# Another order of the graph layers, two of them prepared late, and shared pieces of two graphs from the 17th step on

## The chip, the core and the metric

The kernel runs on one core of a Trainium2 chip. The core has five engines, each with its own in-order queue: PE (TensorE, matmuls and transposes), DVE (VectorE), ACT (ScalarE), POOL (GpSimd) and SP (SyncE, which starts DMAs). They meet only at semaphores: an instruction waits until a counter has reached a constant. The metric is the time of one execution on the device, in microseconds (us), as the median of several runs. All times below are in us unless marked otherwise.

## What is computed

Four graphs of 256 nodes each go through two graph attention layers, then through a mixture of experts. `_L0_xattn_ref` is the attention part, `_L0_ffn_ref` the experts.

```python
def gat_layer(x, adj, W, a_self, a_neigh, b):       # 256 nodes, 8 heads of 32
    feat = jnp.einsum('nf,hfo->hno', x, W)
    attn_self = jnp.einsum('hno,ho->hn', feat, a_self)
    attn_neigh = jnp.einsum('hno,ho->hn', feat, a_neigh)
    e = jax.nn.leaky_relu(attn_self[:, :, None] + attn_neigh[:, None, :], 0.2)
    e = e + MASK_VAL * (1.0 - adj)[None, :, :]
    alpha = jax.nn.softmax(e, axis=-1)
    out = jnp.einsum('hnm,hmo->hno', alpha, feat) + b[:, None, :]
    return jax.nn.elu(jnp.transpose(out, (1, 0, 2)).reshape(out.shape[1], -1))

x = x + jnp.tanh(g_xattn[0]) * two_gat_layers(ctx_512, adj=_layernorm(x))
x = x + jnp.tanh(g_ffn[0]) * experts(_layernorm(x))
```

`experts` picks for each of the 1024 tokens two of eight experts by a router, and adds two shared experts through which every token goes (gate and up projection to 640, silu, product, down projection).

## The kernel before

**The stream of steps.** A layer of a graph is cut into four steps (`UNITS = 4`): two halves of the rows by two groups of four heads. `ORDER` lists the eight pairs (graph, layer) in the order in which they run; L is the place in it, and step w = 4 L + u belongs to layer place L. There are 32 steps (0 to 31). In a second layer the input is the first layer's output of the same graph, `h0_t[n]`. What one step needs of each engine:

- PE: `scores` makes the attention scores (bf16, in ps_z), `turn` transposes the exponentiated scores (8 transposes, ps_pt), `weigh` multiplies them with the features (ps_o).
- ACT: `copy_scores` copies ps_z to SBUF, `exponent` takes four exponentials with row sums, `copy_turned` copies ps_pt.
- DVE: `mask_max` applies the leaky relu and mask and takes the row maxima (one wide instruction and four custom ones).

The work of a step overlaps with that of others: PE makes the scores of step w + 4 while it turns step w, ACT copies the scores of step w + 3 and exponentiates step w + 1, DVE takes the maxima of step w + 3.

**Once per layer.** `score_nodes` (PE, ps_t) and `split_scores` (DVE, three bf16 parts) prepare the scores, `features` (PE, ps_f) and `copy_features` (ACT) the features: one layer ahead. At the end of a layer `invert_sums` (DVE), `spread_inverse` (PE, ps_f), `copy_inverse` (ACT), then `divide` (DVE), `elu_exponent` (ACT) and `end_elu` (DVE) give its output, in steps 0 and 1 of the next layer. Behind a second layer come `turn_h1` (PE), `add_attention` and `normalise` (DVE, with a power on POOL), `turn_x_norm` (PE) and `copy_x_norm` (ACT), then the routing: `router` (PE), `router_exponent` (ACT), `choose` twice (DVE), `ranks` (PE) and `place` (DVE). POOL then scatters the token rows to the experts' slots in memory (`send_rows`).

**The shared experts as fillers.** Per graph there are ten pieces (`PIECES`): `gate_up` on PE (eight matmuls in the trace), a tanh on ACT and two products on DVE (`silu_up`), which write `hidden`. Four down steps (`down`, ten matmuls in the trace) follow. `filler_slots` puts two of these a step between the parts of the attention steps. Graph 0's fourteen slots stood in steps 21 to 28, each piece in the one bank ps_gu, so that a piece waits for the DVE products of the piece before it (`hid_ready`). Graph 1's first five pieces stood in steps 29 to 31, its other five and its downs behind the loop, and these rotated through three banks (ps_gu and the halves of ps_z), which are free since scores come only up to step 27's slot; there a piece waits only for the third piece before it. Behind the loop graphs 2 and 3 follow with all their pieces and downs. Between them stand the small steps of routing.

**Then the routed experts.** 23 tiles of 128 tokens go through gate, up and down with the weights of their expert (`step`, `gate_chunk`, `down_tile`). PE's first routed matmul ends the part that this change touches. It needs the table of tiles (`make_table`, DVE), a tile read back from memory, and the weights of all experts; five experts' weights are loaded late, since their place in SBUF holds the attention's buffers until graph 3 is normalised and the rows of graphs 0 and 1 are sent.

`mask_stats` (DVE) and `make_mask` (POOL) make a graph's mask; `project_second` (DVE) makes the projected attention vectors of the second layers.

## Time and profile before

| | us |
|---|---|
| median of 3 runs | 446.31 (446.15 to 446.85) |
| profiled execution, its own time | 445.5 |
| span of its trace | 443.7 |
| start of the turn of step 17 | 95.00 |
| start of the turn of step 21 (first filler step) | 111.88 |
| start of the turn of step 29 | 171.20 |
| end of the last weigh (step 31) | 187.60 |
| first routed matmul on PE | 267.02 |
| PE busy | 395.6, 89% of the span |

The trace is of one execution. The span leaves out what lies around the first and last instruction, so the execution's own time is 1.8 longer. A line of it names the engine, the source line (L598 is line 598), the operation, what it writes and reads, and how long the engine had stood idle before it and for whom it had waited. Busy time of PE is a little too large, since the modelled ends of matmuls overlap the next start; starts are the better ruler. The names in the rows are those of the tensors in the program, and most of the attention's buffers lie in `weights`.

### The profile page before, as it was taken

Reading aid. Unit: us, or ns where it says so; the run is one execution under the profiler, and the core shown is the slowest. Engines: PE = TensorE matmul, PEld = TensorE weight load, DVE = VectorE, ACT = ScalarE, POOL = GpSimd, SP = SyncE. Lnnn points to the kernel's source line nnn. Section 1 sums busy time; section 2 is a strip of 40 time slices with the busy share of each in tenths; the row PEclk is TensorE's granted clock in tenths of the full one; section 3 lists DMA queues with packets and bytes.
Section 4 is the critical chain, followed back from the end, with each engine's and each line's share of the span. In section 5 each row is a group of like instructions: output and inputs, shape, how many; then the busy total and the mean of one; then the engine's idle time right before and its main releaser. Section 6 shows DMA issues by size and latency. Waiting matters only on the chain.

```text
span 443.7 us, 7225 instructions
## 1 busy us (share of the span) xinstructions
PE 395.6 (89%) x2295; PEld 289.1 (65%) x2296; DVE 257.2 (58%) x814; ACT 205.5 (46%) x519; POOL 90.5 (20%) x100
## 2 busy tenths in 40 slices
PE   3877787787988999997999999999999999999991
PEld 2445464555765878776888886666667676766660
DVE  3799999899887784785474424343333333433330
ACT  4597999999854668420120213232232323232320
POOL 6656140001000022121312000212121212121221
PEclk9998999999998999998999999999999999999997
DMA  6199999100000001000698300122212222221212
GB/s 172 27 353 343 339 354 429 60 1 1 1 1 1 2 7 67 1 24 27 242 429 347 88 2 24 26 36 38 36 38 39 35 46 33 39 36 24 24 12 24
DMA packets 22988, 42.48 MB, mean 96 GB/s; under 512 B 1968, under 2 KB 20976, under 8 KB 21680
## 3 DMA queue, kind: packets, MB, share of 16 engines
q1 hardware_dynamic: 17632, 35.76, 23.3%
q0 software_dynamic: 4080, 5.18, 7.4%
q10 hardware_dynamic: 1248, 1.18, 0.8%
q8 instruction: 16, 0.26, 0.2%
q14 instruction: 12, 0.10, 0.1%
HBM read 24.81 MB, written 17.31 MB: 95 GB/s over the span
## 4 chain that ended last, share of the span: by engine, by line
PE 59%; DVE 19%; ACT 14%; POOL 3%; issue 2%; DMA 2%; POOLq 0%; DVEq 0%
PE ps_z L749 13%; PE ps_o L775 11%; PE ps_gu L749 9%; ACT weights L843 6%; PE ps_pt L605 5%; PE ps_z L598 5%; DVE weights L1041 5%; PE ps_gu L598 4%; DVE weights L1036 3%; ACT weights L834 3%; ACT weights L849 3%; PE ps_pt L765 3%; PE ps_gu L605 2%; DVE hidden L1094 1%; DVE gate_silu L1091 1%
## 5 line engine op out<-in xcount | busy, mean ns | idle before, releaser
L439 POOL DMA_INDIRECT out<-y_sb,tile_in x23 | 35.9, 1559 | 166.1 <-DVE y_sb L1280 163.0
L843 ACT ACTIVATE weights<-weights 128x256 f32<-128x256 f32 x128 | 64.3, 536 | 0.1
L749 PE MATMUL ps_z<-weights,tile_t 128*128 x184 | 63.2, 486 | 0.0
L775 PE MATMUL ps_o<-weights,hidden 128*128 x230 | 53.5, 380 | 0.9 <-ACT hidden L950 0.9
L1091 DVE SCALAR_TENSOR_TENSOR gate_silu<-gate_tanh,ps_z 128x256 f32<-128x256 f32 x66 | 24.5, 371 | 49.5 <-ACT gate_tanh L935 36.2
L517 PE MATMUL ps_pt<-ident,weights 128*128 128x128 f32 x256 | 35.4, 284 | 15.6 <-ACT weights L849 15.2
L749 PEld LDWEIGHTS ps_z<-weights,tile_t 128*128 128x128 f32 x184 | 33.2, 190 | 23.2 <-issue 22.0
L775 PEld LDWEIGHTS ps_o<-weights,hidden 128*128 128x128 f32 x230 | 43.6, 190 | 7.0 <-issue 1.1
L935 ACT ACTIVATE gate_tanh<-ps_gu 128x256 f32<-128x256 f32 x23 | 8.8, 383 | 80.5 <-PE ps_gu L749 80.5
L517 PEld LDWEIGHTS ps_pt<-ident,weights 128*128 128x128 f32 x256 | 29.9, 147 | 22.6 <-issue 21.8
L1036 DVE SCALAR_TENSOR_TENSOR weights<-weights 128x1024 f32<-128x1024 f32 x32 | 39.0, 1219 | 9.1 <-ACT weights L834 5.6
L1091 DVE SCALAR_TENSOR_TENSOR gate_silu<-gate_tanh,ps_gu 128x256 f32<-128x256 f32 x43 | 18.0, 420 | 45.2 <-ACT gate_tanh L935 35.3
L749 PE MATMUL ps_gu<-weights,tile_t 128*128 x92 | 43.2, 592 | 0.0
L598 PE MATMUL ps_gu<-x_norm_t,weights 128*128 128x256 f32 x160 | 39.6, 391 | 4.1 <-DVE hidden L1094 4.1
L834 ACT ACTIVATE weights<-ps_z 128x1024 f32<-128x1024 f32 x32 | 33.5, 1047 | 8.7 <-PE ps_z L508 8.7
L598 PE MATMUL ps_z<-x_norm_t,weights 128*128 128x256 f32 x160 | 37.3, 382 | 0.0
L598 PEld LDWEIGHTS ps_gu<-x_norm_t,weights 128*128 128x128 f32 x160 | 29.7, 192 | 9.1 <-DVE hidden L1094 5.6
L386 POOL TENSOR_TENSOR weights<-weights,minus_half 128x2 f32<-128x2 f32 x8 | 7.5, 940 | 132.3 <-DVE weights L1010 132.3
L849 ACT ACTIVATE weights<-ps_pt 128x1024 f32<-128x1024 f32 x32 | 33.5, 1046 | 0.8 <-PE ps_pt L517 0.8
L598 PEld LDWEIGHTS ps_z<-x_norm_t,weights 128*128 128x128 f32 x160 | 29.8, 190 | 4.1 <-issue 0.4
L935 ACT ACTIVATE gate_tanh<-ps_z 128x256 f32<-128x256 f32 (+1 forms) x46 | 15.2, 330 | 34.7 <-PE ps_z L749 34.7
L505 PE MATMUL ps_z<-weights 96*128 96x512 bf16 x64 | 27.3, 426 | 4.3 <-DVE weights L1026 2.9
(192 smaller groups left out, 618.4 us busy)
## 6 DMA issues: line engine op xcount, KB each, us to landing
weights<-w_experts SPq DMA_DIRECT2D x8, 1920.0 KB, 14.1
slots<-pad_row SPq DMA_DIRECT2D x9, 1188.0 KB, 13.5
weights<-w_experts SPq DMA_DIRECT2D x1, 3840.0 KB, 14.5
tile_in<-slots SPq DMA_DIRECT2D x23, 132.0 KB, 2.1
out<-y_sb ACTq DMA_DIRECT2D x4, 256.0 KB, 2.2
weights<-x SPq DMA_DIRECT2D x2, 256.0 KB, 4.4
x_in<-x SPq DMA_DIRECT2D x2, 256.0 KB, 5.3
out<-y_sb,tile_in POOLq DMA_INDIRECT x23, 3.8
```

Of the source, the lines that this page charges most:

```text
L439: pool.indirect_dma_start(out=out, out_offset=bass.IndirectOffsetOnAxis(ap=tile_in[:, slot, ID_COL:ID_COL + 1].bitcast(U32), axis=0), in_= ...
L505: pe.matmul(ps_z[:, pair, :], v[0:PART_ROWS, half * P:(half + 1) * P], pick_self[0:PART_ROWS, h:h + 2, :], start=True, stop=False, skip_gr ...
L517: mm = pe.transpose(ps_pt[:, i * P:(i + 1) * P], logits[:, w % AHEAD, i * P:(i + 1) * P], ident)
L598: mm = pe.matmul(dst[:, part * N:(part + 1) * N], weights[:, a:a + P], x_norm_t[n % PAIR][:, k, :], start=(k == 0), stop=(k == KC - 1))
L605: mm = pe.matmul(dst, hid_shared[:, e, i, half * P:(half + 1) * P], weights[:, a:a + D], start=(e == 0 and i == 0), stop=(e == NSH - 1 and ...
L749: mm = pe.matmul(ps_chunk[c][:, 0:2 * cw], tile_t[:, r % 2, k, :], weights[:, bass.ds(off + (k * GU + 2 * c0), 2 * cw)], start=(k == 0), s ...
L775: mm = pe.matmul(ps_o[:, 0:D], hid_t[:, r % 2, i, :], weights[:, bass.ds(off + (KC * GU + i * D), D)], start=(i == 0), stop=(i == IC - 1))
L834: act.activation(logits[:, w % AHEAD, :], ps_z.rearrange("p a n -> p (a n)"), ACT.Copy).then_inc(z_copied, 1)
L843: ins = act.activation(v, v, ACT.Exp, bias=neg_max[:, w % AHEAD, i:i + 1], scale=-1.0, accum_out=sums[:, L % PAIR, s:s + 1])
L849: act.activation(probs_t[:, w % 2, :], ps_pt, ACT.Copy).then_inc(probs_copied, 1)
L1036: dve.scalar_tensor_tensor(out=z, in0=z, scalar=LEAK, in1=z, op0=ALU.mult, op1=ALU.max).then_inc(bent_ready, 1)
L1091: dve.scalar_tensor_tensor(out=gate_silu[:, s, 0:w], in0=gate_tanh[:, s, 0:w], scalar=1.0, in1=gate, op0=ALU.add, op1=ALU.mult).then_inc(r ...
```

## The change

`ORDER` becomes 00 10 01 20 11 30 21 31 (graph, layer), so that graph 0's second layer stands at place 2 rather than 3 and graph 1's at place 4 rather than 5. At places 2 and 7 a second layer now follows its own first layer with only one other between them. These two are `TIGHT`: their `score_nodes`, `split_scores` and `features` come in the steps right before them, and their scores are made two steps later than those of other layers, with their copies and maxima squeezed in behind. Graph 0's filler slots move from steps 21 to 28 to steps 17 to 24. Graph 1's thirteen first slots stand in steps 25 to 31, now all in the bank ps_gu as graph 0's, and one down step is left behind the loop. Behind the loop the small steps of routing are spread anew between the pieces of graph 2, and the ranks, place and table of graph 3 move behind the first pieces of graph 3. The statistics of graphs 2 and 3 move to steps 5 and 10, the second projection to step 1.

```diff
-ORDER = ((0, 0), (1, 0), (2, 0), (0, 1), (3, 0), (1, 1), (2, 1), (3, 1))
+ORDER = ((0, 0), (1, 0), (0, 1), (2, 0), (1, 1), (3, 0), (2, 1), (3, 1))
+TIGHT = tuple(L for L in range(2, STREAM) if ORDER[L][1] == 1 and ORDER[L - 2] == (ORDER[L][0], 0))
+NODES_AT = {UNITS * L - 3 if L in TIGHT else UNITS * (L - 1) - 1: L for L in range(PAIR, STREAM)}
+FEATURES_AT = {UNITS * L - 2 if L in TIGHT else UNITS * L - 3: L for L in range(PAIR, STREAM)}
+SPLIT_AT = {UNITS * L - 2 if L in TIGHT else UNITS * (L - 1): L for L in range(PAIR, STREAM)}
 def filler_slots(w):
     if w < FIRST_FILL:
-        return ()
-    if w < SECOND_FILL:
-        first = 2 * (w - FIRST_FILL) - 1
-        return tuple((0, s) if 0 <= s < PIECES + len(DOWNS) else None for s in (first, first + 1))
-    first = 2 * (w - SECOND_FILL) - 1
-    return tuple((1, s) if s >= 0 else None for s in (first, first + 1))
+        return None, None
+    n, at = (0, FIRST_FILL) if w < SECOND_FILL else (1, SECOND_FILL)
+    first = 2 * (w - at) - 1
+    return tuple((n, s) if 0 <= s < PIECES + len(DOWNS) else None for s in (first, first + 1))
+def scores_early(w):
+    if tight_step(w, -1):
+        return w + 2
+    if tight_step(w, 0):
+        return w + 3
+    return w + 4 if w % UNITS != 0 and is_free(w + 4) else None
+def scores_late(w):
+    if tight_step(w, -2):
+        return w + 2
+    if tight_step(w, -1):
+        return w + 3
+    return w + 4 if w % UNITS == 0 and is_free(w + 4) else None
...
# the loop on PE
-                if slots_now and slots_now[0]:
-                    filler(slots_now[0])
-                if u != 0 and w + UNITS < ALL_UNITS:
-                    scores(w + UNITS)
+                if first:
+                    filler(first)
+                if scores_early(w) is not None:
+                    scores(scores_early(w))
...
# the loop on ACT
-                if w + 3 < ALL_UNITS:
-                    copy_scores(w + 3)
+                if copy_early(w) is not None:
+                    copy_scores(copy_early(w))
...
+                if tight_step(w, -1):
+                    copy_turned(w)
+                    copy_scores(copy_late(w))
                 if w + 1 < ALL_UNITS:
                     exponent(w + 1)
-                if slots_now and slots_now[0] and slots_now[0][1] < PIECES:
-                    tanh_piece(*slots_now[0], piece_bank(*slots_now[0]))
+                if first and first[1] < PIECES:
+                    tanh_piece(*first, 0)
...
# behind the loop on DVE
             for n in range(PAIR, B):
                 for i in range(PIECES):
                     tail_piece(n, i)
-                    if n == PAIR and i == 6:
+                    if n == 3 and i == 0:
                         place(3, ps_o)
-                    if n == PAIR and i == 7:
+                    if n == 3 and i == 1:
                         make_table()
```

`tight_step(w, k)` is true where w lies k steps from the first step of a tight layer, `is_free` where a step belongs to no tight layer; `copy_early`, `copy_late` and `maxima` hold the same kind of table for ACT's copies and DVE's maxima. `turn_bank_free` holds the waits on the bank ps_t that stood in three places.

**The first tight layer, on ACT.** These are ACT's rows of steps 5 to 7, and the copy that opens step 8. ps_z is read by `copy_scores`, weights<-weights x4 is `exponent`, ps_pt is read by `copy_turned`, ps_f by `copy_features`. Before:

```order
L834 ACTIVATE weights<-ps_z 128x1024
L843 ACTIVATE weights<-weights 128x256 x4
L860 ACTIVATE att_exp<-weights 128x256 x2
L849 ACTIVATE weights<-ps_pt 128x1024
L834 ACTIVATE weights<-ps_z 128x1024
L830 ACTIVATE weights<-ps_f 128x512
L843 ACTIVATE weights<-weights 128x256 x4
L849 ACTIVATE weights<-ps_pt 128x1024
L834 ACTIVATE weights<-ps_z 128x1024
```

After:

```order
L888 ACTIVATE weights<-weights 128x256 x4
L905 ACTIVATE att_exp<-weights 128x256 x2
L894 ACTIVATE weights<-ps_pt 128x1024
L888 ACTIVATE weights<-weights 128x256 x4
L894 ACTIVATE weights<-ps_pt 128x1024
L879 ACTIVATE weights<-ps_z 128x1024
L875 ACTIVATE weights<-ps_f 128x512
L894 ACTIVATE weights<-ps_pt 128x1024
L879 ACTIVATE weights<-ps_z 128x1024
L888 ACTIVATE weights<-weights 128x256 x4
```

Steps 5 and 6 lose their copies of scores, and step 7 has two, with the copy of its turned weights between them and the exponents of step 8 behind.

**The second tight layer, on ACT.** Before, these are the rows of steps 29 (from its tanh) to 31 (up to its first tanh), with the pieces of graph 1 (gate_tanh):

```order
L876 ACTIVATE gate_tanh<-ps_gu 128x256
L880 DMA out<-y_sb 128x2x256
L843 ACTIVATE weights<-weights 128x256 x4
L876 ACTIVATE gate_tanh<-ps_z 128x256
L849 ACTIVATE weights<-ps_pt 128x1024
L876 ACTIVATE gate_tanh<-ps_z 128x256
L876 ACTIVATE gate_tanh<-ps_gu 128x256
```

After, the rows of steps 27 and 28, with pieces 3 to 5 of graph 1:

```order
L879 ACTIVATE weights<-ps_z 128x1024
L875 ACTIVATE weights<-ps_f 128x512
L894 ACTIVATE weights<-ps_pt 128x1024
L879 ACTIVATE weights<-ps_z 128x1024
L888 ACTIVATE weights<-weights 128x256 x4
L921 ACTIVATE gate_tanh<-ps_gu 128x256 x2
L879 ACTIVATE weights<-ps_z 128x1024
L900 ACTIVATE weights<-ps_f 128x512
L888 ACTIVATE weights<-weights 128x256 x4
L921 ACTIVATE gate_tanh<-ps_gu 128x256
L894 ACTIVATE weights<-ps_pt 128x1024
L879 ACTIVATE weights<-ps_z 128x1024
```

The first tanh of step 27 stands behind two copies of scores, a copy of features, a copy of turned weights and four exponents, and all pieces are in ps_gu.

**Behind the loop, on PE.** The counts are those of the program, half of the trace's. L598 (before) and L653 (after) are pieces, L605 and L660 downs, L566 and L621 the turn of graph 3's attention output, L543 and L598 (after) the turn of its normalised rows. Before:

```order
L598 MATMUL ps_gu<-x_norm_t1,weights 128x256 x4
L566 MATMUL ps_t<-ident,weights 128x128 x4
L598 MATMUL ps_z<-x_norm_t1,weights 128x256 x4
L578 MATMUL ps_f<-router_w,x_norm_t0 128x8 x4
L598 MATMUL ps_z<-x_norm_t1,weights 128x256 x4
L598 MATMUL ps_gu<-x_norm_t1,weights 128x256 x4
L543 MATMUL ps_t<-ident,rows30 128x128 x4
L605 MATMUL ps_pt<-weights,hidden 128x256 x10
```

After:

```order
L660 MATMUL ps_gu<-weights,hidden 128x256 x5
L653 MATMUL ps_z<-x_norm_t0,weights 128x256 x4
L621 MATMUL ps_t<-ident,weights 128x128 x4
L653 MATMUL ps_z<-x_norm_t0,weights 128x256 x4
L633 MATMUL ps_f<-router_w,x_norm_t0 128x8 x4
L653 MATMUL ps_gu<-x_norm_t0,weights 128x256 x4
L653 MATMUL ps_z<-x_norm_t0,weights 128x256 x8
L598 MATMUL ps_t<-ident,rows30 128x128 x4
```

The pieces between the small steps are now graph 2's (x_norm_t0), one more of them stands between the turn of the attention output and the turn of the rows, and of graph 1 (x_norm_t1) only one down step is left in front.

## Rows read from the trace of the kernel before

**Rows 1.** Busy time by stretch: engines in us, granted clock, share of DMA.

```profile
95.00:111.88 16.88, 14.13 (x144) 10.46 (x145) 16.05 (x49) 16.88 (x45) 1.32 (x2) 1.00 0.01 1
111.88:171.20 59.32, 55.17 (x405) 43.37 (x404) 44.58 (x155) 38.24 (x100) 5.69 (x6) 0.97 0.03 10
171.20:187.60 16.40, 16.23 (x147) 13.09 (x145) 10.89 (x34) 10.58 (x29) 1.28 (x2) 1.00 0.05 17
187.60:267.02 79.42, 75.43 (x369) 65.31 (x366) 42.56 (x163) 12.42 (x33) 13.11 (x15) 0.98 0.42 162
267.02:443.70 176.68, 166.31 (x666) 112.27 (x664) 61.73 (x162) 46.23 (x114) 35.85 (x23) 0.98 0.21 32
```

**Rows 2.** Chain of work that ended last, six pieces of it: start, us, what.

```profile
63.97 0.80 ACT att_exp L860 x2
...
67.06 1.97 ACT weights L843 x8
69.03 0.91 ACT weights L849
...
120.41 1.24 DVE weights L1036
121.67 1.47 DVE weights L1041 x8
...
217.48 1.73 PE ps_gu L598 x8
...
265.02 2.16 PE ps_pt L605 x10
```

**Rows 3.** Timeline of PE in step 17: start, us, line, operation, idle before.

```profile
95.00 1.06 PE L517 MATMUL ps_pt<-ident,weights 128*128 128x128 f32 x8 [1.29 <-ACT weights L849]
95.90 0.38 PE L505 MATMUL ps_z<-weights 96*128 96x512 bf16 x1
...
96.87 0.65 PE L532 MATMUL ps_o<-weights 128*32 128x128 f32 x16
97.44 1.99 PE L490 MATMUL ps_f<-w_sb,weights 128*128 128x256 f32 x8
```

**Rows 4.** Timeline of DVE, the first piece of graph 0.

```profile
119.49 0.42 DVE L1091 SCALAR_TENSOR_TENSOR gate_silu<-gate_tanh,ps_gu 128x256 f32<-128x256 f32 x1 [1.59 <-ACT gate_tanh L876]
```

**Rows 5.** Timeline of DVE (first row) and ACT in steps 1 to 5.

```profile
32.88 0.75 DVE L1005 BATCH_NORM_STATS2 weights<-x_in 128x6 f32<-128x256 f32 x2
...
36.87 1.03 ACT L834 ACTIVATE weights<-ps_z 128x1024 f32<-128x1024 f32 x1
39.62 0.60 ACT L855 ACTIVATE weights<-ps_f 128x512 f32<-128x512 f32 x1 [1.72 <-PE ps_f L557]
...
42.43 1.03 ACT L849 ACTIVATE weights<-ps_pt 128x1024 f32<-128x1024 f32 x1 [0.26 <-PE ps_pt L517]
44.10 1.02 ACT L834 ACTIVATE weights<-ps_z 128x1024 f32<-128x1024 f32 x1 [0.64 <-PE ps_z L508]
```

**Rows 6.** Timeline of PE around three of its stops.

```profile
140.00 2.78 PE L598 MATMUL ps_gu<-x_norm_t,weights 128*128 128x256 f32 x8 [1.99 <-DVE hidden L1094]
142.58 0.63 PE L505 MATMUL ps_z<-weights 96*128 96x512 bf16 x1
...
201.94 0.66 PE L543 MATMUL ps_t<-ident,rows 128*128 128x128 f32 x4 [3.12 <-DVE rows L1085]
202.44 6.17 PE L605 MATMUL ps_pt<-weights,hidden 128*128 128x256 f32 x20
...
236.48 4.58 PE L605 MATMUL ps_pt<-weights,hidden 128*128 128x256 f32 x20 [0.66 <-DVE hidden L1094]
```

**Rows 7.** Timeline of DVE: place of graph 3, table, and the next piece.

```profile
227.57 0.15 DVE L1139 TENSOR_TENSOR top_r<-best 128x2 f32<-128x2 f32 x1
...
230.26 0.41 DVE L1091 SCALAR_TENSOR_TENSOR gate_silu<-gate_tanh,ps_z 128x256 f32<-128x256 f32 x1
...
231.05 0.16 DVE L1159 TENSOR_TENSOR fill_r<-next_row,ramp_region 128x8 f32<-128x8 f32 x1
...
234.77 0.41 DVE L1091 SCALAR_TENSOR_TENSOR gate_silu<-gate_tanh,ps_gu 128x256 f32<-128x256 f32 x1
```

More of the change, by code:

```diff
@@ L61 @@
 AHEAD = 4
-def layers_before(L, layer):
-    return sum(1 for n, l in ORDER[:max(L, 0)] if l == layer)
+TIGHT = tuple(L for L in range(2, STREAM) if ORDER[L][1] == 1 and ORDER[L - 2] == (ORDER[L][0], 0))
 def second_layer(L):
@@ L76, in step_after, with done_before @@
     return UNITS * (ORDER.index((n, 1)) + 1) + steps
+def done_before(table, w):
+    return sum(1 for at in table if at < w)
+TURN_H1 = {step_after(n, 2): n for n in range(B)}
 TURN_X_NORM = {step_after(n, UNITS): n for n in range(PAIR)}
@@ L674, in _ @@
                 if w in COPY_X_NORM:
                     router(COPY_X_NORM[w], ps_t)
-                if w == PLACE_FIRST:
-                    pe.wait_ge(parts_ready, STREAM)
-                    ranks(0, ps_t)
-                if slots_now and slots_now[1]:
-                    filler(slots_now[1])
+                if w in PLACE:
+                    turn_bank_free(w, PAIR + done_before(SPLIT_AT, w + 1))
+                    ranks(PLACE[w], ps_t)
+                if second:
+                    filler(second)
@@ L729, in _ @@
                 shared_piece(3, i)
+                if i == 0:
+                    pe.wait_ge(ranks_read, 3)
+                    ranks(3, ps_o)
             def turn_in(q, r):
```

228 lines of the change are left out of this document (119 added, 109 removed).

## The prediction, made before the changed kernel had run

> **What bounds the kernel now.** I read the stretches first: PE, ACT and DVE busy time from step 17 (at 95.00 us) to the first routed matmul (at 267.02 us). They show three regimes [rows 1]. In steps 17 to 20 ACT is busy for all of 16.88 us and PE for 14.13: ACT sets the pace. In steps 21 to 28, which carry the filler pieces of graph 0, PE is busy for 55.17 of 59.32 us. Behind the loop PE is busy for 75.43 of 79.42 us. From 267.02 on the code is the same in both kernels and takes 176.68 us.
>
> The chain of waits says the same for the loop: one step on ACT is copy of scores, exponents, copy of turned weights, with the ELU exponent once a layer [rows 2]. Four steps take 16.87 us on ACT with no gap. So a filler put among steps that ACT paces is free only as far as PE stands idle there, and the whole question is where PE idles before and after. PE's own work is nearly the same in both kernels.
>
> The prices: a gate and up piece 1.73, a down step 2.16 (ten matmuls in the trace) [rows 2], by the starts a turn 0.90, a step's scores some 0.9 and a weigh 0.57, features of a second layer 1.9 [rows 3]. On DVE a piece costs two instructions of 0.42 [rows 4], and a mask maximum 1.24 and then 1.47, some 2.65 with their overlap [rows 2].
>
> **Part 1, the start and the first tight layer (steps 1 to 12).** DVE had the statistics of graph 2 in step 1 and the second projection in step 2, both ahead of the inversion that PE and ACT wait for. The statistics (1.14 us) go to step 5 [rows 5]. ACT's copy of the inverse, which stood 1.72 us at 39.62, can then follow its own copy of scores at 37.8: 1.8 us gained. Against that, layer 2 is now the second layer of graph 0, whose input is ready only with the end of the ELU in step 5. By ACT's queue: ELU exponent done 44.0, end of ELU on DVE 44.7, node scores on PE (four matmuls) 45.6, turn 46.5, weigh 47.1, features 48.9, scores of step 8 at 49.8, so ACT copies them at 49.9, having been free from 47.75. That stop is 2.15. The exponent of step 8 then waits for a 2.65 us maximum behind 2.3 us of other copies: 0.5. In step 9 ACT asks for scores of step 12 that PE could not start before ACT's last copy: 1.0, a full round trip. The stops of before in the same stretch, 0.26 and 0.64 [rows 5], go (the stop of 1.72 is in the 1.8). Sum: -1.8 + 3.65 - 0.9 = **+1.0**, and 0.3 more in steps 16 and 17, where the split on DVE comes late. Turn 17 starts at 96.3 instead of 95.00. Bounds: -0.9 (no stop) and +4 (the low clock falls on PE while ACT waits for it).
>
> **Part 2, steps 17 to 24.** These carry the same fourteen fillers, at the same distance from the layers, as steps 21 to 28 before. Only the features at step 17 are of a first layer, half as long: -0.8. So 59.32 - 0.8 = 58.5, and step 25 starts at 154.8. This is where the change gains: the like point of the fillers, step 29, came at 171.20 before [rows 1], and seven steps instead of three are left, among which to spread graph 1.
>
> **Part 3, steps 25 to 31, with thirteen fillers of graph 1 in one bank and the second tight layer.** Here I follow the queues. Steps 25 and 26: turn 0.9, weigh 0.57, router 0.9, piece 1.75, node scores 0.9, turn 0.9, piece 1.75, weigh 0.57, features 1.85, piece 1.75, scores 0.87: 12.8 with the small waits. Call the end of the scores of step 28 zero. In step 27 ACT now has, one after another, copy of scores 28, features, turned weights, copy of scores 29 (which PE makes behind a piece, ready at 3.5), the exponents of 28, and only then the tanh of piece 3. Piece 3 was ready at 2.6; its tanh ends at 6.8 and DVE's half at 7.7. All pieces use ps_gu, so piece 4 may not start before that. PE has been free from 4.1: **a stop of 3.65**. Piece 4 ends at 9.5, its DVE half at 10.7, and the maximum of step 29 stands behind it on DVE, so the exponents of 29 start at 13.4, the tanh of piece 5 ends at 15.7 and DVE, after a second maximum, frees the bank at 16.9: PE free from 14.9, a stop of 2.0. In step 29 two stops of 0.5 and 1.1; in step 30 1.1 and 0.9. Then downs, which don't wait. Zero to the end of the last weigh: 39.8. Steps 25 to the last weigh: 12.8 + 39.8 = **52.6**, of which some 9 is idle. The last weigh ends at 96.3 + 58.5 + 52.6 = 207.4; before it ended at 187.6 [rows 1].
>
> Before, the pieces of graph 1 stood in steps 29 to 31 where no scores were left, and rotated through three banks, and PE was busy for 16.23 of 16.40 us [rows 1]. That cover is gone.
>
> **Part 4, behind the loop.** It was 79.42. Five pieces leave (5 x 1.73 = 8.65) and three down steps (3 x 2.16 = 6.48). The stop of 3.12 before the turning of graph 3 goes [rows 6], since the normalising has POOL to itself and two pieces stand before the wait; also the 0.66 before the downs of graph 2, and the ranks of graph 1 (0.1). The stretch with the lower clock behind the 3.12 stop (20 matmuls took 6.17 where they take 4.5) goes too: 1.7. What comes late instead: place and table now stand on DVE behind the first two pieces of graph 3, 2.7 and 3.7 us long [rows 7]. With a piece's half done 3.2 after its start, then 2.7, 0.85, 3.7 and 0.85, the third piece's half is done at 11.3, and the sixth piece waits for it from 8.8: +2.5. Before, the same two stood behind pieces 6 and 7, and the downs covered them. Sum: 79.42 - 8.65 - 6.48 - 3.12 - 0.66 - 0.1 - 1.7 + 2.5 = **61.2**. The tiles are in time: rows of graph 3 go out 5.9 after that first piece starts, while PE needs the first tile some 26 after it.
>
> **Sum.** 207.4 + 61.2 = 268.6 for the first routed matmul. **The clock.** Before, PE stopped for 1.99 at 138.0 and its next score matmuls took 0.63 instead of 0.38, and after the 3.12 stop the same [rows 6]: the granted clock was at 1.2 GHz, not 2.4, for a stretch, at 1.7 us each. Stops such as the 1.29 between ACT-paced steps had no such mark [rows 3]. The new kernel has stops of 3.65, 2.0 and 2.5; I take one such stretch, +1.7 (bounds 0 and 5.1). So 270.3 against 267.02: +3.3. On the profiled execution, 445.5 (span 443.7), that gives 448.8; its own time is 0.8 under the median of 446.31, and on the median it is **449.6**.
>
> The Trainium skill (TensorE: Matmul & The Clock Gate, the two states of the clock) speaks against this last term: it lets the clock fall after an idle window, not for a short stop, and the stops that I forecast are short. This case's row of the 1.99 stop disagrees. By the page the term would be 0 and the sum 447.9.
>
> **Rivals.**
> 1. The clock holds. If the stops of part 3 and 4 fall so that no stretch at 1.2 GHz follows, and the one at 141 us goes as well: 449.6 - 1.7 - 1.7 = 446.2 to 447.9, say 447.4. For it: the shorter stops, which had no mark. Against: both stops above 1.9 in this stretch had one. The rule named above is this rival. Chance 0.2.
> 2. Faster: the chain of step 27 is no chain. If PE idles in steps 25 to 31 as in steps 21 to 28 (4.15 of 59.32 us, so some 3.2 in 45), the 9 of part 3 fall by 5 to 6, and the clock term with them: 449.6 - 5.5 - 1.7 = 442.4. It decides on whether the tanh of piece 3 gets onto ACT before the exponents of step 28; the order says no. Between it and my sum lies a middle case, near 445, where half of the stops are covered. Chance 0.17 together.
> 3. No change: part 1 costs nothing (startup gain kept, the stops hidden behind DVE's lead) and one of the stops of part 3 is short: near 446.3. Chance 0.13.
> 4. Slower still: each of the three stops brings its stretch of low clock, and part 1 another: 449.6 + 3.4 = 453. Chance 0.1.
> My forecast, 448.3 to 451.5: 0.4.
>
> **The numbers.** A comparison of these kernels can tell about 0.2% (0.9 us) from no change. Slower by more than that: my forecast 0.4, rival 4 0.1, most of rival 1 0.15: 0.65. Same: rival 3 and the rest of rival 1, 0.17. Faster: rival 2 and a little of 3, 0.18. The range from 443.5 to 453.0 leaves out the far end of rival 2 and what lies beyond rival 4.
>
> **What would show it.** Turn 17 should start between 96 and 97 us; ACT should show a wait for PE of about 2 us before the copy of scores 8. Step 25 at 155, the last weigh at 207, the first routed matmul at 270. Among PE's waits the one on DVE's hidden should grow from 4.1 in six waits to some 11, with a longest near 3.6 in the step that turns the 28th weights. The wait for rows from POOL should be gone, and the sixth piece of graph 3 should wait 2.5. I am wrong if no stop above 2.5 stands before a piece of graph 1, or if turn 17 starts before 95.

## The result, and the profile after

| | before | after |
|---|---|---|
| median | 446.58 (446.15 to 447.72, 4 runs) | 454.13 (448.98 to 454.31, 4 runs) |
| profiled execution, its own time | 445.5 | 454.31 |
| span of its trace | 443.7 | 452.5 |
| mean granted clock, of full speed | 0.982 | 0.965 |

The ratio after to before is 1.015, with a 95% interval of 1.011 to 1.019. That is 6.7 us slower (5.0 to 8.4) by the ratio and 7.5 by the medians. The forecast was +3.3, 449.6 with a range up to 453.0: the direction was right, the size less than half.

The waits of PE in the trace of after: who waits, on whom, total us, times, longest.

```profile
PE ps_gu L653 <- DVE hidden L1144: 11.8, 11, 3.7
PE ps_pt L572 <- ACT weights L894: 7.4, 6, 2.2
...
PE ps_z L560 <- ACT weights L879: 4.8, 4, 2.7
PE ps_z L653 <- DVE hidden L1144: 2.3, 1, 2.3
```

The first row is the single bank of the pieces: 11.8 us where before it was 4.1 in six waits. The last is the wait of the sixth piece of graph 3. No wait for rows from POOL is left; it was the 3.12 of [rows 6].

Busy time by stretch in after, cut at turn 17, turn 25, the end of the last weigh (213.71) and the first routed matmul (275.74), the last two cuts rounded; columns as in [rows 1].

```profile
99.34:158.00 58.66, 54.50 (x401) 42.44 (x400) 44.59 (x155) 38.28 (x100) 5.70 (x6) 0.97 0.03 10
158.00:214.00 56.00, 47.41 (x360) 37.45 (x359) 33.04 (x112) 29.87 (x78) 5.26 (x6) 0.97 0.04 13
214.00:275.00 61.00, 58.75 (x287) 51.06 (x286) 34.74 (x131) 10.42 (x27) 9.11 (x10) 0.97 0.53 204
```

In the middle one PE stands idle for 8.6 of 56 us. In the stretch of before in which graph 1's first pieces stood it was idle for 0.17 of 16.40 [rows 1].

The forecast had the stops of PE. These are its rows of steps 27, 28, 29 and 30 and of the sixth piece of graph 3, with the stop of step 20 ahead of them, which the old order has in its step 24 (timeline of PE; start, duration, in brackets the idle time before).

```profile
126.80 2.96 PE L653 MATMUL ps_gu<-x_norm_t,weights 128*128 128x256 f32 x8 [1.98 <-DVE hidden L1144]
...
178.93 3.63 PE L653 MATMUL ps_gu<-x_norm_t,weights 128*128 128x256 f32 x8 [3.67 <-DVE hidden L1144]
...
190.03 1.99 PE L653 MATMUL ps_gu<-x_norm_t,weights 128*128 128x256 f32 x8 [2.10 <-DVE hidden L1144]
193.47 1.99 PE L653 MATMUL ps_gu<-x_norm_t,weights 128*128 128x256 f32 x8 [0.58 <-DVE hidden L1144]
...
200.99 1.99 PE L653 MATMUL ps_gu<-x_norm_t,weights 128*128 128x256 f32 x8 [0.78 <-DVE hidden L1144]
...
256.46 5.41 PE L653 MATMUL ps_z<-x_norm_t,weights 128*128 128x256 f32 x16 [2.25 <-DVE hidden L1144]
```

Forecast 3.65, 2.0 and 2.5 for the three large ones; measured 3.67, 2.10 and 2.25. What the forecast did not have stands in the second column. Eight matmuls of a piece take 1.9 to 2.0 us at full clock and took 3.63 behind the stop of 3.67. Two pieces take 3.6 and took 5.41 behind the stop of 2.25. That is PE at 1.2 GHz. Behind the stop of 2.10 the piece took 1.99: there the clock held. Behind the 1.98 of step 20 it fell, as it did before behind the 1.99 of step 24.

The same happens twice in the first thirteen steps (timeline of PE; turn 5, weigh 4, node scores of layer 2, turn 6, then scores of step 12 and turn 9).

```profile
41.14 1.06 PE L572 MATMUL ps_pt<-ident,weights 128*128 128x128 f32 x8 [2.20 <-ACT weights L894]
42.77 1.08 PE L587 MATMUL ps_o<-weights 128*32 128x128 f32 x16 [0.57 <-issue]
44.70 1.99 PE L531 MATMUL ps_t<-weights,wa_sb 128*96 128x256 f32 x4 [0.85 <-DVE weights L1120]
46.49 1.91 PE L572 MATMUL ps_pt<-ident,weights 128*128 128x128 f32 x8
...
63.40 0.59 PE L560 MATMUL ps_z<-weights 96*128 96x512 bf16 x1 [2.72 <-ACT weights L879]
...
65.06 1.92 PE L572 MATMUL ps_pt<-ident,weights 128*128 128x128 f32 x8
```

The turn at 41.14 takes 1.06, as at full clock; the weigh at 42.77 takes 1.08 where others take 0.65, and the turn at 46.49 takes 1.91. So the clock fell within 2 us behind the stop of 2.20 (at 42.3 by the records), before the 0.85 came. From 63.40 to 68.05 every instruction of PE takes about twice its time. What ACT, which sets the pace here, paid for it (timeline of ACT: copies of turned 6, of scores 8 and of scores 12):

```profile
48.44 1.02 ACT L894 ACTIVATE weights<-ps_pt 128x1024 f32<-128x1024 f32 x1 [1.80 <-PE ps_pt L572]
52.19 1.03 ACT L879 ACTIVATE weights<-ps_z 128x1024 f32<-128x1024 f32 x1 [2.73 <-PE ps_z L563]
...
65.30 1.02 ACT L879 ACTIVATE weights<-ps_z 128x1024 f32<-128x1024 f32 x1 [2.05 <-PE ps_z L563]
```

The forecast had ACT's stops as 0, 2.15 and 1.0. The profile page's row of the clock in 40 slices, of before and then of after:

```profile
PEclk9998999999998999998999999999999999999997
```

```profile
PEclk9998879999989999999999899999999999999996
```

The records behind the row have the clock at 1.2 GHz in three stretches of before (near 40, 141 and 202 us) and in five of after (near 45, 66, 127, 179 and 257 us), of which the first two last twice as long as the others: seven lengths against three. The double ones are the 8, 8 and 7 in slices 4 to 6. Both kernels have one more at the very end. Over the span, (1 - 0.965) x 452.5 x 2 = 31.7 us of after ran at half clock, against (1 - 0.982) x 443.7 x 2 = 16.0 before.

### The profile page after: what moved, and what is told of

It is laid out like the page before. It is cut to its first block, busy times and chain, and to the rows that moved or that the text cites. A ratio compares the mean times of both kernels' runs of the same rounds, so it can differ in the third digit from the quotient of the medians.

```text
span 452.5 us, 7229 instructions
## 1 busy us (share of the span) xinstructions
PE 403.0 (89%) x2295; PEld 293.4 (65%) x2296; DVE 256.7 (57%) x814; ACT 206.2 (46%) x519; POOL 88.6 (20%) x100
## 4 chain that ended last, share of the span: by engine, by line
PE 68%; DVE 14%; ACT 13%; DMA 2%; issue 1%; POOL 0%; DVEq 0%; POOLq 0%
PE ps_z L794 13%; PE ps_o L820 10%; PE ps_gu L794 9%; PE ps_gu L653 7%; ACT weights L888 6%; PE ps_z L653 5%; PE ps_gu L660 4%; PE ps_pt L660 4%; ACT weights L879 4%; DVE weights L1091 3%; PE ps_pt L810 3%; DVE weights L1086 3%; ACT weights L894 2%; PE ps_z L560 2%; PE ps_f L545 2%; PE ps_pt L572 2%
## 5 line engine op out<-in xcount | busy, mean ns | idle before, releaser
L653 PE MATMUL ps_gu<-x_norm_t,weights 128*128 128x256 f32 x208 | 53.4, 402 | 11.8 <-DVE hidden L1144 11.8
L1141 DVE SCALAR_TENSOR_TENSOR gate_silu<-gate_tanh,ps_gu 128x256 f32<-128x256 f32 x49 | 20.6, 420 | 56.2 <-ACT gate_tanh L985 35.3
L653 PEld LDWEIGHTS ps_gu<-x_norm_t,weights 128*128 128x128 f32 x208 | 39.2, 198 | 19.2 <-DVE hidden L1144 14.5
L1141 DVE SCALAR_TENSOR_TENSOR gate_silu<-gate_tanh,ps_z 128x256 f32<-128x256 f32 (+1 forms) x60 | 22.0, 367 | 43.6 <-ACT gate_tanh L985 36.2
L1086 DVE SCALAR_TENSOR_TENSOR weights<-weights 128x1024 f32<-128x1024 f32 x32 | 39.0, 1220 | 11.8 <-ACT weights L879 8.1
L572 PE MATMUL ps_pt<-ident,weights 128*128 128x128 f32 x256 | 37.1, 293 | 7.8 <-ACT weights L894 7.4
L572 PEld LDWEIGHTS ps_pt<-ident,weights 128*128 128x128 f32 x256 | 31.9, 152 | 13.0 <-issue 11.0
L560 PE MATMUL ps_z<-weights 96*128 96x512 bf16 x64 | 28.7, 449 | 6.9 <-ACT weights L879 4.8
L653 PE MATMUL ps_z<-x_norm_t,weights 128*128 128x256 f32 x112 | 27.5, 399 | 2.3 <-DVE hidden L1144 2.3
L1331 DVE TENSOR_SCALAR y_sb<-ps_o,tile_in 128x256 f32<-128x256 f32 x23 | 11.1, 484 | 31.9 <-PE ps_o L820 31.9
## 6 DMA issues: line engine op xcount, KB each, us to landing
slots<-pad_row SPq DMA_DIRECT2D x9, 1188.0 KB, 13.7
```

What stands on the lines that cost most here:

```text
L560: pe.matmul(ps_z[:, pair, :], v[0:PART_ROWS, half * P:(half + 1) * P], pick_self[0:PART_ROWS, h:h + 2, :], start=True, stop=False, skip_gr ...
L572: mm = pe.transpose(ps_pt[:, i * P:(i + 1) * P], logits[:, w % AHEAD, i * P:(i + 1) * P], ident)
L653: mm = pe.matmul(dst[:, part * N:(part + 1) * N], weights[:, a:a + P], x_norm_t[n % PAIR][:, k, :], start=(k == 0), stop=(k == KC - 1))
L1086: dve.scalar_tensor_tensor(out=z, in0=z, scalar=LEAK, in1=z, op0=ALU.mult, op1=ALU.max).then_inc(bent_ready, 1)
L1141: dve.scalar_tensor_tensor(out=gate_silu[:, s, 0:w], in0=gate_tanh[:, s, 0:w], scalar=1.0, in1=gate, op0=ALU.add, op1=ALU.mult).then_inc(r ...
```

## The experiments

**The theories.** A: the loss is two things of like size, the stops of the queues as forecast, and PE's low clock behind them, above all in the first thirteen steps, where ACT waits for PE. B: the low clock only shows where PE has time to spare, and the whole loss is longer queues: idle time given to PE would change nothing. C: the single bank, not ACT's order, makes the stops of steps 27 to 30. Where idle transposes are put in, they transpose the identity matrix into a bank that is free just then, and their result is read by nobody.

**1. PE kept busy in steps 4, 5 and 8 of the changed kernel.**

```diff
+EARLY_BUSY = {4: 14, 5: 8, 8: 20}
...
+            def keep_busy(bank, count):
+                for i in range(count):
+                    pe.transpose(bank[:, (i % 4) * P:(i % 4 + 1) * P], ident, ident)
...
                 if w > 0:
                     weigh(w - 1)
+                if w in EARLY_BUSY:
+                    keep_busy(ps_gu, EARLY_BUSY[w])
```

> The new kernel with 14, 8 and 20 transposes of the identity put on PE in steps 4, 5 and 8, where it stands idle before the first tight layer's scores; their result is not used. Nothing else changes. Theory (the clock): part 1 came out 3.0 us longer than worked out (turn 17 at 99.34 instead of 96.3) because PE ran at 1.2 GHz in two stretches there (44.7 to 49 and 63 to 69.5 us). With PE kept busy the granted clock stays at 2.4 GHz in both, the copy of scores 8 starts near 50 instead of 52.19, turn 17 starts between 96 and 97, and the time falls by 3 to 5 us, to 449 to 451. Rival (the queues): the added length comes from waits that were worked out too short; then the transposes change nothing, turn 17 stays at 99.3 and the time at 454, or it grows by what they delay.

Measured: 450.64 (449.8 to 452.23), ratio to before 1.010 (1.007 to 1.013). 3.5 us came back by the medians, for 42 more transposes on PE. The median of after rests on four runs, one of them at 448.98, and the intervals of the two ratios touch; the traces are the stronger evidence. The granted clock of the stretch from 34 to 99 us, before, after and in this run:

```profile
34.00:99.00 65.00, 49.84 (x497) 34.64 (x496) 60.66 (x191) 62.38 (x165) 13.25 (x8) 0.97 0.75 257
```

```profile
34.00:99.00 65.00, 50.60 (x467) 34.83 (x465) 57.22 (x181) 57.95 (x152) 12.70 (x10) 0.89 0.74 254
```

```profile
34.00:99.00 65.00, 53.03 (x532) 37.95 (x533) 59.36 (x191) 60.61 (x158) 12.74 (x10) 1.00 0.75 256
```

0.97, 0.89, 1.00; and ACT gets 60.61 us of work done there instead of 57.95. The two traces are level up to turn 5 (41.14 and 41.27); turn 17 starts at 96.92 instead of 99.34. The stop of 2.72 before the scores of step 12 is filled but for 0.39. That this isn't one lucky execution is seen in the other traces: with the early part left as it is (after, experiments 2 and 3) turn 17 starts at 98.55 to 99.34, with it filled (experiments 1, 4, 5, 9 and 11) at 96.55 to 97.36. B falls.

The experiments below are read by the same marks, in us (the "last weigh" is its end):

| | turn 17 | turn 17 to 25 | turn 25 to last weigh | last weigh to first routed | first routed |
|---|---|---|---|---|---|
| after | 99.34 | 58.66 | 55.71 | 62.03 | 275.74 |
| experiment 1 | 96.92 | 58.65 | 55.68 | 62.04 | 273.29 |
| experiment 2 | 98.55 | 58.67 | 51.64 | 62.04 | 270.90 |
| experiment 3 | 98.66 | 58.67 | 55.65 | 57.82 | 270.80 |
| experiment 4 | 97.36 | 58.07 | 54.07 | 60.35 | 269.85 |
| experiment 5 | 96.55 | 56.97 | 52.46 | 57.83 | 263.81 |

**2. In step 27, the tanh of piece 3 ahead of the copy of scores and the exponents.**

```diff
                 if tight_step(w, -1):
                     copy_turned(w)
+                    if first and first[1] < PIECES:
+                        tanh_piece(*first, 0)
                     copy_scores(copy_late(w))
                 if w + 1 < ALL_UNITS:
                     exponent(w + 1)
-                if first and first[1] < PIECES:
+                if first and first[1] < PIECES and not tight_step(w, -1):
                     tanh_piece(*first, 0)
```

> The new kernel with ACT's tanh of the first filler piece of step 27 moved ahead of the copy of scores 29 and the exponents of step 28. Theory (ACT's queue): the stop of 3.67 us in step 27 is that tanh standing behind a copy and four exponents; with it moved, the piece's DVE half comes right behind the maximum of step 28, PE's stop falls to about 1 us, the low clock behind it goes, and the time falls by 2.5 to 4.5 us against the new kernel, to 450 to 451.5. Rival (the single bank): the stop is the bank's, since piece, tanh and products take turns in ps_gu and DVE is held by the maxima; then the stop only moves to the next piece and the time falls by less than 1 us.

Measured: 450.54 (448.5 to 451.74), ratio 1.010 (1.007 to 1.013): 3.6 less. PE's row of piece 4:

```profile
175.72 1.99 PE L653 MATMUL ps_gu<-x_norm_t,weights 128*128 128x256 f32 x8 [1.24 <-DVE hidden L1146]
```

The stop goes from 3.67 to 1.24 and the piece from 3.63 to 1.99: 2.4 of queue and 1.7 of clock, by moving one instruction of 0.38 us; from turn 25 to the last weigh it is 4.1 less. The stop of step 28 is still 2.11. So the order on ACT's queue makes most of the stop of step 27, as the forecast had it, and C is wrong for this one.

The same trace shows a fall of the clock that after does not have, at turn 11:

```profile
72.09 1.94 PE L572 MATMUL ps_pt<-ident,weights 128*128 128x128 f32 x8 [1.75 <-ACT weights L894]
```

Stops of 1.74 and 1.75 between ACT-paced steps left the turn behind them at 1.06 or 1.07 in the kernel before, and so did most of them in other runs. But here, and in experiments 7, 8 and 10, one or two of them were followed by the low clock.

**3. Ranks, place and table of graph 3 back behind the last piece of graph 2.**

```diff
 # PE
                 shared_down(2, e, half)
+                if e == 0 and half == HV - 1:
+                    pe.wait_ge(ranks_read, 3)
+                    ranks(3, ps_o)
             for i in range(PIECES):
                 shared_piece(3, i)
-                if i == 0:
-                    pe.wait_ge(ranks_read, 3)
-                    ranks(3, ps_o)
 # DVE
-                    if n == 3 and i == 0:
+                    if n == 2 and i == 9:
                         place(3, ps_o)
-                    if n == 3 and i == 1:
                         make_table()
```

> The new kernel with ranks, place and table of graph 3 taken from behind the first pieces of graph 3 back behind the last piece of graph 2, where four down steps cover them. Theory (cover lost): the stop of 2.25 us before the sixth piece of graph 3 and the stretch at 1.2 GHz behind it (16 matmuls in 5.41 us where they take 3.6) both go: 4 us less, 450.1. Rival: what it saves is taken back by the downs of graph 2 or by the saving of its base, which then stands behind the table on DVE: no change, 454.

Measured: 449.86 (449.31 to 450.01), ratio 1.008 (1.006 to 1.010): 4.3 less. The pieces of graph 3 now run without a stop:

```profile
246.41 1.89 PE L653 MATMUL ps_gu<-x_norm_t,weights 128*128 128x256 f32 x8
248.13 3.62 PE L653 MATMUL ps_z<-x_norm_t,weights 128*128 128x256 f32 x16
251.59 1.89 PE L653 MATMUL ps_gu<-x_norm_t,weights 128*128 128x256 f32 x8
```

2.25 of stop and 5.41 - 3.62 = 1.8 of clock are 4.05; the stretch behind the last weigh is 4.2 shorter.

**4. PE kept busy in all the large stops.** As the first, with 14 more idle transposes in step 20, 26 in step 27, 14 in step 28 and 14 before the sixth piece of graph 3. The stops stay; only the clock can change.

> As e1, and also transposes of the identity on PE in four later stops: 14 in step 20, 26 in step 27, 14 in step 28 and 14 before the sixth piece of graph 3, each shorter than the stop. The clock theory expects all stretches at 1.2 GHz but those at the start to go, each worth about 1.7 us of the matmuls behind it: three more than e1, so 5 us less than e1, 444 to 446, though the stops themselves stay. The rival (stops alone) expects no gain over e1. A gain of 1 to 3 us over e1 would mean that part of the low-clock time is hidden behind other engines.

Measured: 447.10 (446.37 to 448.15, 12 runs), ratio 1.001 (1.000 to 1.003); mean clock 0.990 in the profiled run. That is 3.5 under the first experiment, where 5 was expected, and 7.0 under after, with nothing removed from the kernel. Its row in the table has both the gain and the miss. The stretches of steps 20 and 27 and of graph 3's sixth piece are gone, and each gave 1.6 to 1.7, as expected. But the clock now falls once at 96.4, behind a stop of 1.71 before the scores ahead of turn 17, which no other trace has: that took back 0.4 at turn 17 and 1.1 behind it (58.07 where experiment 5 has 56.97).

The Trainium skill (TensorE: Matmul & The Clock Gate, HAM oscillation) takes the cost of a low clock as the time spent in it times (1 - 1.2/2.4). By it, an estimate, going from 0.965 of 452.5 us to 0.990 of 446.4 us (31.7 to 8.9 us at half clock) would be worth 11.4; the run gave 7.0. The trace agrees on the three late stretches (10.2 us at half clock, 5.1 by the rule, 5.0 given back). For the two double ones in the ACT-paced part the rule is too high: 13.7 us at half clock, 6.8 by the rule, 2.4 at turn 17. What PE does slowly while ACT has other work costs nothing (the early stretch of the kernel before, in experiment 6, is such a case).

**5. The three cures together** (the first, second and third, with the 14 transposes of step 20).

> The new kernel with e1's transposes in steps 4, 5 and 8, 14 more in step 20, e2's earlier tanh and e3's earlier table. If the four causes are separate, their effects add: against e1's 450.6, some 2.4 for the stop of step 27, 1.8 for the clock behind it, 4.0 for the table's stop and its clock and 1.7 for step 20 give 440.7, below both kernels. The rival (each stop only moves to the next wait) expects 444 or more, since a chain through ps_gu in steps 28 to 30 would take back what step 27 gives.

Measured: 442.47 (441.54 to 443.58), ratio 0.991 (0.988 to 0.994). 11.7 of after's time is gone. In the traces it is 11.9, and the parts add up: 2.8 at turn 17, 1.7 in step 20, 3.3 for the tanh, 4.2 for the table. Of the miss of 1.8 against the forecast some 0.8 has a row (52.46 where experiment 2 has 51.64): the stop of step 28 is 2.10 as before, but now the clock falls behind it.

```profile
181.46 2.74 PE L656 MATMUL ps_gu<-x_norm_t,weights 128*128 128x256 f32 x8 [2.10 <-DVE hidden L1163]
```

In experiment 2 the same stop of 2.11 had no such mark. So the length of a stop alone doesn't decide. In the traces the first routed matmul is 9.5 earlier than in experiment 1, of 9.9 forecast. The rest of the miss lies in the medians: the profiled execution of experiment 1 took 451.67, its median is 450.64.

**6. The kernel before, kept busy in its three stops** (18 transposes in step 3, 14 in step 24, 22 before the turn of graph 3's rows). It gives the old order the same treatment as experiment 4 gives the new.

> The kernel before with transposes of the identity on PE in its own three long stops: 18 in step 3, 14 in step 24, 22 before the turning of graph 3's rows behind the loop. The stops stay, the three stretches at 1.2 GHz should go. Clock theory: 1.7 for each of the two in PE-bound stretches and 1 for the one at the start, 4 to 4.5 us less than before, 442. It says what the new order costs at equal clock: e4 (447.1) has the same treatment, so the order itself would be 5 us slower. The rival, that the order costs nothing and all 8 us are clock, expects this run within 1 us of e4.

Measured: 442.36 (441.68 to 443.50), ratio 0.991 (0.988 to 0.994): 4.0 less. So at a clock that is held nearly everywhere the new order costs 447.1 - 442.4 = 4.7, and of the loss of 7.5 some 3 is clock. That division is good to about 1, since each of the two kernels has one low stretch left: in this one the clock falls at 61.4, behind stops of 1.06 and 0.52, and turn 17 starts at 95.86 instead of 95.00. The transposes of step 3 gave nothing (turn 5 at 43.88, before at 43.90), so the early stretch of the kernel before had been free. In the traces the gain comes from the other two, 1.7 each. So both parts of A are there, the one somewhat larger than the other.

**7. The kernel before, graph 3's power on POOL ahead of sending the rows of graph 1.**

```diff
+                power(B + n, n % PAIR)
                 if n == 3:
                     send_rows(1)
-                power(B + n, n % PAIR)
                 copy_rows(n)
```

> The kernel before with POOL's power for graph 3 put ahead of the sending of graph 1's rows (one change of order on POOL). Expected: PE's stop of 3.12 us behind the loop and the low clock behind it go, 3.0 and 1.7 us, 441.5. This is the one part of the changed kernel's gain that was forecast in part 4 (4.8 us) done alone. If the time stays above 444, that term was not a real gain, for example since the late rows then come later.

Measured: 442.14 (441.11 to 443.60), ratio 0.990 (0.987 to 0.993). The gain that the new order makes behind the loop, the stop of 3.12 [rows 6], is to be had by a swap of two lines on POOL:

```profile
201.08 0.66 PE L543 MATMUL ps_t<-ident,rows 128*128 128x128 f32 x4 [0.20 <-DVE rows L1085]
201.58 4.48 PE L605 MATMUL ps_pt<-weights,hidden 128*128 128x256 f32 x20
```

The twenty down matmuls that took 6.17 take 4.48, and from the last weigh to the first routed matmul it is 74.86 instead of 79.43: 4.6 less, with 4.7 expected.

**8. The kernel before with both** (POOL's swap, and the transposes of steps 3 and 24).

> e7 with e6's transposes in steps 3 and 24. Expected 2.7 less than e7 if the clock's terms and the stop add: 438.8, the fastest of all. If the phase of the clock decides more than the stops, it will scatter by 1.7 or more between runs.

Measured: 439.72 (438.92 to 441.68), ratio 0.986 (0.983 to 0.989): 2.4 less than experiment 7, where 2.7 was expected.

**9. Two more banks for graph 1** in the kernel of experiment 5: pieces 7 and 8 (step 29) go to the halves of ps_z.

```diff
 def piece_bank(n, i):
+    if n == 1 and i in (7, 8):
+        return i - 6
...
-                    if piece > 0:
+                    if n == 1 and piece == 7:
+                        pe.wait_ge(z_copied, ALL_UNITS)
+                    elif n == 1 and piece == 9:
+                        pe.wait_ge(hid_ready, PIECES + 7)
+                    elif piece > 0 and (n, piece) != (1, 8):
                         pe.wait_ge(hid_ready, PIECES * n + piece)
-                    gate_up(n, piece, ps_gu)
+                    gate_up(n, piece, ps_chunk[piece_bank(n, piece)])
```

> The new order with idle transposes, tanh of step 27 first and table early (the version that took 442.47), and pieces 7 and 8 of graph 1 (step 29) put into the two halves of ps_z, which are free once the scores of step 31 are copied; piece 9 is back in ps_gu. If the single bank is the cause of the stops of 0.59, 0.78 and 0.81 before pieces 8, 9 and the first down, the first two go and the third stays near 0.8 or shrinks to 0.4: 1.4 to 1.8 less, some 440.9. The stop of 2.10 before piece 6 stays, since ps_z still holds scores then. Rival: the exponents and maxima of steps 29 to 31 set the pace, and the turns wait for ACT instead: then the stops move to the turns of steps 30 and 31 and the time stays at 442.5.

Measured: 440.16 (439.09 to 441.26), ratio 0.986 (0.983 to 0.989): 2.3 less than experiment 5. PE in steps 28 to 30 (pieces 6, 8 and 9):

```profile
182.03 2.77 PE L658 MATMUL ps_gu<-x_norm_t,weights 128*128 128x256 f32 x8 [2.10 <-DVE hidden L1169]
...
188.95 1.97 PE L658 MATMUL ps_z<-x_norm_t,weights 128*128 128x256 f32 x8
...
192.07 1.89 PE L658 MATMUL ps_gu<-x_norm_t,weights 128*128 128x256 f32 x8
```

Pieces 8 and 9 have no stop, and no turn waits in their place; the stop before the first down step stays at 0.81, as expected. C holds for the small stops of pieces 7 to 9. The stop of 2.10 is as it was. Its six runs fall in two groups: three at a clock of 0.995 took 439.1 to 439.7, three at 0.984 to 0.989 took 440.7 to 441.3. The profiled one is of the second group and shows a stretch at 1.2 GHz behind the stop of 2.10, and one near 26 us.

**10. The kernel before, the first seven pieces of graph 1 in one bank.** This takes away the cover that the prediction named.

```diff
-    return (PIECES * (n - 1) + i) % 3 if n > 0 else 0
+    return (PIECES * (n - 1) + i) % 3 if n > 1 or n == 1 and i > 6 else 0
...
-                if m >= 3:
+                if 0 < m < 7:
+                    pe.wait_ge(hid_ready, PIECES + m)
+                elif m >= 7:
```

> The kernel before, with the first seven pieces of graph 1 (steps 29 to 31 and the two behind the loop) all in ps_gu, each waiting for the DVE half of the piece before it. If the three banks were the cover that the prediction names, PE now stops before pieces 1 to 6, for 0.3 to 1 each: +3, about 449.5, and the last weigh ends 2 to 3 later than at 187.6. Rival: turns and weighs between the pieces cover the wait anyway and only adjacent pieces stop: +1 or less.

Measured: 447.48 (445.82 to 451.24, 12 runs), ratio 1.003 (1.000 to 1.006): +1.1, nearer to the rival's +1 than to +3. In the trace the stops are there, before pieces 2, 3, 4 and 6 (the first and the last of them, then the turn of graph 3's rows):

```profile
181.88 2.00 PE L598 MATMUL ps_gu<-x_norm_t,weights 128*128 128x256 f32 x8 [0.81 <-DVE hidden L1096]
...
196.53 1.99 PE L598 MATMUL ps_gu<-x_norm_t,weights 128*128 128x256 f32 x8 [1.35 <-DVE hidden L1096]
...
207.05 0.66 PE L543 MATMUL ps_t<-ident,rows 128*128 128x128 f32 x4 [2.00 <-DVE rows L1087]
207.54 4.48 PE L605 MATMUL ps_pt<-weights,hidden 128*128 128x256 f32 x20
```

They are 0.81, 1.59, 0.81 and 1.35, 4.56 together. But DVE's rows of graph 3 don't move as far, so the stop of 3.12 shrinks to 2.00, and the 20 matmuls behind it run at full clock: 1.1 + 1.7 of the 4.56 come back. The profiled execution is 3.4 above that of before all the same, with a clock of 0.975. Of this 1.4 stands ahead of the edited code (turn 29 at 172.62, before at 171.20), where it has three low stretches more than before had; 2.0 stands behind it. Of the twelve runs the three at 0.991 took 445.8 to 446.2, and the one at 0.971 took 451.2. The cover was real (the last weigh ends 3.6 later, counted from turn 29); its worth in the old order is small, 1.1 by the medians and 2.0 in the trace, since the wait for POOL stood behind it.

**11. The ninth, with 14 transposes before the second piece of step 28.**

> The version with two more banks, plus 14 idle transposes into ps_f before the second piece of step 28, where a stop of 2.10 had brought a stretch at 1.2 GHz. If that stretch is the clock's doing and nothing else, it goes: 1.5 less than the version without them, some 439.5, as fast as the best of the old order (439.72). Rival: the clock falls elsewhere instead, and the time stays.

Measured: 439.58 (438.78 to 441.08), ratio 0.985 (0.982 to 0.988). The piece's row, with the transposes that fill the stop:

```profile
179.51 1.75 PE L695 MATMUL ps_f<-ident 128*128 128x128 f32 x14
181.68 2.00 PE L658 MATMUL ps_gu<-x_norm_t,weights 128*128 128x256 f32 x8 [0.42 <-DVE hidden L1169]
```

2.77 becomes 2.00, as expected, and from turn 25 to the last weigh it is 49.38 instead of 50.59. By the medians the gain is 0.6, not 1.5, which six runs of each can't tell from nothing. A likely reason, not tested apart, is that three of the ninth's six runs had a clock of 0.995 already and so no such stretch to lose. The new order with its cures is as fast as the old one with its own (439.58 and 439.72); neither beats the other by more than can be measured.

## Why the prediction was wrong in size

| point | forecast | measured in after | same point, clock held |
|---|---|---|---|
| turn 17 | 96.3 | 99.34 | 96.92 (experiment 1) |
| turn 17 to turn 25 | 58.5 | 58.66 | |
| turn 25 to end of last weigh | 52.6 | 55.71 | |
| last weigh to first routed matmul | 61.2 | 62.03 | |
| first routed matmul | 270.3 | 275.74 | 269.85 (experiment 4), with one stretch of its own, some 1.5 |

**The step that failed** is the term of the clock, "I take one such stretch, +1.7 (bounds 0 and 5.1)". The new stretches cost 5.8 in the trace: 2.4 in part 1, 1.7 in step 27 and 1.7 behind the stop of graph 3's sixth piece. The stops themselves were forecast well.

**Part 1** gave +1.0 and 0.3, worked out with PE at full speed. With the clock held turn 17 starts at 96.92. Before it started at 95.00, and that trace's early stretch cost nothing (experiment 6), so the layer order as such cost 1.9: the +1.3 was 0.6 too low. The other 2.4 are the clock. The sum counted how long ACT would stand and never asked how long PE had stood before it: PE's stops of 2.20 and 2.72 are what ACT-paced steps look like on PE. The forecast's sentence on such stops, that they had no mark, rested on one of 1.29. The trace of before already had a mark in this part, behind a stop of 2.66, and the forecast doesn't name it; the instructions behind it take 1.04 where they take 0.66 at full clock:

```profile
38.54 1.04 PE L557 MATMUL ps_f<-ident,weights 128*128 128x128 f32 x4 [2.66 <-DVE weights L1049]
```

The bound of +4 named this case ("the low clock falls on PE while ACT waits for it"). The three executions with the early part unfilled came to +3.6, +3.7 and +4.3, so what was kept as a bound was the usual case.

**Part 2** was right to 0.2: same fillers at the same distance cost the same, the stretch behind the stop of 1.98 among it.

**Part 3.** The stops were right: 3.65 and 2.0 against 3.67 and 2.10, and the four small ones, forecast as 0.5, 1.1, 1.1 and 0.9, came as 0.58, 0.65, 0.78 and 0.81. Experiment 2 shows the cause of the first, experiment 9 that of the small ones but the last. Of the 3.1 too much, 1.7 is clock behind the first stop (3.63 for a piece of 1.9). PE's own work was added up some 2.0 too low, and the stops together were 0.7 shorter than forecast.

**Part 4** was near: a stop of 2.25 for 2.5, POOL's stop gone. 62.03 holds 1.8 of clock, so the rest is 1.0 below the 61.2.

**The clock over the whole.** The forecast left the stretches in steps 3 and 24 of the old order as they were, took one away behind the loop and added one: three, where after has seven lengths. By experiments 4 and 6 holding the clock is worth 7.0 in after and 4.0 in before, so the clock costs 3.0 more than before, and the rest of the change 4.7. In the traces the first routed matmul comes 8.7 later than before: some 4.1 of that is clock (7.5 in after, 3.4 in before) and 4.6 the rest. The forecast's sum had the one at 0 (one stretch gone, one new) and the other at +3.3; the rest was too low by the 0.6 of part 1 and the 2.0 of PE's work in part 3, and too high by 0.7 of stops there and 1.0 in part 4. Rival 4, each of the three stops with its own stretch and one more in part 1, was 453 and came nearest to the median of 454.1; of its three stops two had the stretch, and part 1 had two double ones.

Rival 1, the clock that holds, is what the Trainium skill (TensorE: Matmul & The Clock Gate, the two states of the clock) would have had, idle windows and not short stops; the rows of 2.72 and 2.25 disagree with it as those of before did. The prediction took all of its forecast stops as short by that page of the Trainium skill. For the longest, 3.65, that was too quick: the page's table of advice is against gaps of that length, and the stop of 3.67 had its stretch.

**The spread** is the clock too. The lowest run of after, 448.98, has a mean clock of 0.977 where the other three have 0.965 or 0.966: (1 - 0.977) x 447.2 x 2 = 20.6 us at half clock against 31.7. Half of the 11.1 between them is 5.5, and the run is 5.1 faster. That there are two such groups of the same kernel was seen again in experiment 9; what puts an execution in one or the other no run here shows. Experiment 7 has the same early code as before and turn 17 at 97.03 instead of 95.00, with three low stretches there for one: so two single traces of the same code can differ by 2 us here.

**What stays open.** The 2.0 of PE work in part 3 have no experiment of their own. No experiment removed the stop of 2.10 of step 28; the forecast's account of it (a second maximum ahead of the piece's half on DVE) was not tested. The cost of the tight layers as such, with their fillers left as they were, was not tried. Why the clock falls behind one stop and not behind another of the same length no run shows.

## What to carry to other kernels

Price a stop of the busiest engine twice: for its length, and for what the clock does to the work behind it, and do so also in stretches where another engine sets the pace, since there the slow matmuls land in that engine's waits. Before a queue is reordered for a new schedule, list for each in-order queue what stands ahead of the short instruction that frees a bank: one tanh of 0.38 us was worth 3.6 here. And try the local cure of a wait first: a swap of two lines on POOL gave the old order 4.3, while the new order, which removes the same wait by moving half the program, lost 7.5.

## What the runs showed of the hardware

- TensorE fell from 2.4 to 1.2 GHz behind single stops of 2.20, 2.25, 2.72 and 3.67. Behind the stop of 1.98 or 1.99 in step 20 (step 24 of the old order) it fell in all seven traces that left it unfilled. A stop of 2.10 had the low clock behind it in experiments 5 and 9 and not in after or experiment 2; of the stops of 1.75 a few had it and most had not.
- A piece of 1.9 us behind such a stop took 3.6, two in a row 5.4 instead of 3.6: 1.6 to 1.8 a time where PE is the bound. Where ACT is the bound, two double stretches cost 2.4 at turn 17, and the early one of the kernel before cost nothing.
- Throwaway transposes of the identity in a stop keep the clock: behind none of the filled stops did it fall. 42 of them gave 3.5 us, 110 gave 7.0 (medians). It fell once elsewhere in experiment 4, behind a stop of 1.71, and once in experiment 6, behind stops of 1.06 and 0.52. Placed so that they end before the wait does, the transposes leave a rest of it (0.42 in experiment 11) and delay nothing.
- The mean granted clock of a run explains most of the spread between runs of one kernel: 448.98 at 0.977 and 454.2 at 0.965; 439.3 at 0.995 and 441.0 at 0.987 (means of three).
